# A transformer block on one core: the first batch's root on ScalarE, the second operand set copied, the weights' preparation put later

## The chip, the cores and the metric

The kernel runs on one core of one Trainium2 chip. The metric is the device time of the program in microseconds. The program is one launch that takes all inputs from DRAM and leaves the block's output there.

## What is computed

The reference, cut to what matters (B = 4 batches, T = 1024 tokens, C = 128 channels, 16 heads of 8 channels):

```python
x = x + layernorm(attn(layernorm(x), weight))
x = x + layernorm(ffn(layernorm(x), W_r, W_k, W_v, mu_r, mu_k))

def attn(x, weight):                       # b, t, c = 4, 1024, 128
    y = x.reshape(b, t, 16, 8).transpose(0, 2, 1, 3)
    scores = einsum('bhtk,bhsk->bhts', y, y) / sqrt(8)
    o = einsum('bhts,bsc->bhtc', softmax(scores), x)
    return o.transpose(0, 2, 1, 3).reshape(b, t, 16 * c) @ weight

def ffn(x, W_r, W_k, W_v, mu_r, mu_k):     # x_prev is x moved by one token
    r = sigmoid((mu_r * x + (1 - mu_r) * x_prev) @ W_r.T)
    k = square(relu((mu_k * x + (1 - mu_k) * x_prev) @ W_k.T))
    return r * (k @ W_v.T)
```

## The kernel before

The 4096 tokens are eight rows of 512. A row and a head are a step (128 steps, number j), and a step is two quads of 512 keys (256 quads, number k). All float32 products are made of float16 parts, a rounded value and what it leaves.

Every engine runs its own list, written out by hand over one loop variable k, in which the engines meet by semaphores. In iteration k the work is this:

- TensorE: `score(k)` (four 32-row matmuls into the four banks of `ps_s`), then `products(k - 4)` (twelve matmuls of 512 columns into a bank of `ps_o`), then `project(j)` (twelve matmuls of 128 columns into `ps_r`) in every second iteration. `score(k)` waits until the exponentials of quad k - 1 have left `ps_s`.
- ScalarE: `weigh(k)`, the exponentials of 128x2048 scores into `e_f`; `take_o(j)`, the rounding of a finished `ps_o` bank; `scale(j)`, four divisions of the projected step by its softmax sum.
- GpSimd: `cast(k)`, the issue of a DMA that rounds `e_f` to float16 in `e_hi`. Quad 0 is rounded by VectorE.
- VectorE: `split_quad(k - 2)`, which needs `cast` landed and gives `e_lo`; `split_o(j)`, `invert(j)`, `add(j)`.
- SyncE: all other transfers, above all the operands of the scores, which steps 4 and later read back from a scratch in DRAM. The operands of steps 0 to 3 come from TensorE transposes of `comb_s` and `comb_t`, in two sets (steps 0 and 1, steps 2 and 3).

The opening, which the change touches, does the following beside that pipeline. VectorE forms means and variances of batch 0, its inverse root (`batch_root`, L1017: an integer first guess and three rounds of three instructions, each waiting for the one before), and a negated product for ScalarE's share of the normalization (L1223, semaphore `centred`; ScalarE's `normalize_half`, L857). `first_operands(n)` on VectorE (L1075) builds set n from x: subtract, multiply, round, take the rest, square, sum, root, shift. TensorE's `first_operands(n)` (L531) transposes them, ScalarE's `take_first_s`, `take_first_t` and `take_second_t` (L861 to L876) copy them into `op_s` and `op_t`, and `score(4)` waits for the second set.

The weights of the projection are prepared in the opening as well. TensorE's `weights_less(i)` (L560, float32, 512 columns) subtracts the last row in four parts; VectorE's `weight_base(i)` (L1097) subtracts the last column; `weight_sum` on TensorE (L526), `keep_weight_sum` on ScalarE (L850) and `weight_scale` on VectorE (L1105) find a power of two; ScalarE's `weights_high` and `weights_neg` (L791, L798) and VectorE's `weights_low` (L1116) make the three float16 parts. `project(0)` (L616) waits for all of it. `step_at(k, lead)` (L247) tells in which iteration step j is projected (lead 8 on TensorE), scaled and inverted (lead 9), and added (lead 10): before, step 0 stands at lead + 1, step 1 at lead + 2, step 2 at lead + 4, and so on by two. In iteration 12 the feed-forward weights are turned by TensorE (`turn_ffn_weights`, L573) and copied by ScalarE (`turn_in_ffn_weights`, L877), on both ahead of that iteration's work for steps.

## Time and profile before

| | before |
|---|---|
| median of 3 runs | 944.18 us (943.57 to 948.45) |
| the profiled execution, its own time | 950.29 us |
| its span in the trace | 948.5 us |
| TensorE busy | 914.9 us, 96% |
| VectorE busy | 850.3 us, 90% |
| ScalarE busy | 753.4 us, 79% |
| GpSimd busy | 320.2 us, 34% |
| granted TensorE clock over the span | 0.999 |

The profile is one execution. "Busy" of an engine is the time in which it had an instruction under way. The granted clock is what the throttle let through and is not all that sets the pace: a column of one matmul form can cost twice as much in one stretch as in another, so the duration of a form is read where it stands. Views used: the page with its shares, the timeline of a stretch (start, duration, engine, line, operation, and in square brackets the idle time of the engine before it with its releaser), and the chain of work that ended last in order of time.

### The profile page before, as it was taken

The numbers are of one execution on the slowest core, as the hardware profiler recorded it, in microseconds if no ns is written. First come the engines' busy times: TensorE is split into PE (matmuls) and PEld (weight loads), VectorE is DVE, ScalarE is ACT, GpSimd is POOL, SyncE is SP. The second block draws the span as 40 slices with busy tenths as digits, with TensorE's granted clock in tenths as the row PEclk, the third lists the DMA queues.
The fourth block names the chain that finished last, engine by engine and source line by source line (L and its number), as shares of the span: only waits on it lengthen the run. The fifth ranks groups of instructions, "written<-read, shape, count | busy, mean of one in ns | idle before, by whom it ended". The sixth has DMA issues, their size and how long they took to land.

```text
span 948.5 us, 17874 instructions
## 1 busy us (share of the span) xinstructions
PE 914.9 (96%) x6065; PEld 441.9 (47%) x6065; DVE 850.3 (90%) x1117; ACT 753.4 (79%) x1048; POOL 320.2 (34%) x485
## 2 busy tenths in 40 slices
PE   3999999999999999999999999999999999999995
PEld 2444444444544444444444444544544444444453
DVE  7889898899898899989988979989889899898887
ACT  6787878788778778888778887889787978788855
POOL 2111432441143613515115282443313451153501
PEclk9999999999999999999999999999999999999999
DMA  5899999989889888999988978899988989889840
GB/s 162 195 225 188 205 197 200 226 190 204 177 173 201 163 181 174 208 193 207 185 178 179 203 157 179 176 222 202 206 173 180 188 182 188 172 179 201 174 81 24
DMA packets 98698, 173.12 MB, mean 183 GB/s; under 512 B 21040, under 2 KB 61360, under 8 KB 98608
## 3 DMA queue, kind: packets, MB, share of 16 engines
q0 software_dynamic: 36720, 133.71, 72.3%
q1 hardware_dynamic: 61888, 38.28, 14.7%
q8 instruction: 49, 0.80, 0.3%
q14 instruction: 41, 0.34, 0.1%
HBM read 27.72 MB, written 10.49 MB: 40 GB/s over the span
## 4 chain that ended last, share of the span: by engine, by line
PE 80%; issue 5%; POOL 4%; DVE 4%; DMA 4%; ACT 4%; DVEq 0%; POOLq 0%; ACTq 0%
PE ps_o L610 22%; PE ps_o L612 20%; PE ps_o L611 20%; PE ps_s L591 7%; DMA e_hi<-e_f 3%; PE ps_r L625 3%; PE ps_r L627 3%; PE ps_r L626 3%; ACT e_f L776 2%; DVE e_lo L1129 1%; POOL zT L452 1%; POOL e_hi L433 1%; PE ps_x L652 1%; PE ps_x L648 1%; POOL fnw L411 1%
## 5 line engine op out<-in xcount | busy, mean ns | idle before, releaser
L1129 DVE TENSOR_TENSOR e_lo<-e_f,e_hi 128x2048 f16<-128x2048 f32 x256 | 586.1, 2290 | 62.2 <-DMA e_hi<-e_f 62.1
L776 ACT ACTIVATE e_f<-ps_s 128x2048 f32<-128x2048 f32 x256 | 481.6, 1881 | 133.8 <-PE ps_s L591 124.4
L610 PE MATMUL ps_o<-e_hi,y_hi 128*128 128x512 f16 x1024 | 390.7, 382 | 6.3 <-DVE o_neg L1135 4.7
L612 PE MATMUL ps_o<-e_hi,y_lo 128*128 128x512 f16 x1024 | 388.1, 379 | 0.0
L611 PE MATMUL ps_o<-e_lo,y_hi 128*128 128x512 f16 x1024 | 388.1, 379 | 0.0
L433 POOL DMA_DIRECT2D e_hi<-e_f x255 | 140.9, 553 | 571.1 <-ACT e_f L776 469.8
L610 PEld LDWEIGHTS ps_o<-e_hi,y_hi 128*128 128x128 f16 x1024 | 99.7, 97 | 155.0 <-issue 56.1
L788 ACT ACTIVATE part<-ps_r,rden 128x128 f32<-128x128 f32 x508 | 144.8, 373 | 33.3 <-DVE rden L1141 32.6
L612 PEld LDWEIGHTS ps_o<-e_hi,y_lo 128*128 128x128 f16 x1024 | 100.2, 98 | 120.9
L611 PEld LDWEIGHTS ps_o<-e_lo,y_hi 128*128 128x128 f16 x1024 | 100.4, 98 | 91.5 <-issue 0.7
L591 PE MATMUL ps_s<-op_t,op_s 32*128 32x512 f16 x1024 | 102.5, 388 | 2.9 <-ACT e_f L776 2.4
L625 PE MATMUL ps_r<-w_hi,o_hi 128*128 128x128 f16 x508 | 91.6, 219 | 0.9 <-ACT part L788 0.9
L627 PE MATMUL ps_r<-w_neg,o_neg 128*128 128x128 f16 x508 | 91.6, 219 | 0.0
L626 PE MATMUL ps_r<-w_lo,o_hi 128*128 128x128 f16 x508 | 91.6, 219 | 0.0
L1151 DVE TENSOR_TENSOR acc<-acc,part 128x512 f32<-128x512 f32 x119 | 81.3, 683 | 9.4 <-ACT part L788 8.7
L1135 DVE SCALAR_TENSOR_TENSOR o_neg<-o_hi,ps_o 128x512 f16<-128x512 f16 x127 | 86.0, 677 | 2.3 <-ACT o_hi L781 2.1
L781 ACT ACTIVATE o_hi<-ps_o 128x512 f16<-128x512 f32 x127 | 76.1, 599 | 0.1
L591 PEld LDWEIGHTS ps_s<-op_t,op_s 32*128 32x128 f16 x1024 | 26.3, 91 | 66.7 <-issue 50.5
L625 PEld LDWEIGHTS ps_r<-w_hi,o_hi 128*128 128x128 f16 x508 | 49.7, 98 | 16.5 <-issue 1.9
L626 PEld LDWEIGHTS ps_r<-w_lo,o_hi 128*128 128x128 f16 x508 | 49.7, 98 | 14.6
L627 PEld LDWEIGHTS ps_r<-w_neg,o_neg 128*128 128x128 f16 x508 | 49.7, 98 | 0.0
L1141 DVE RECIPROCAL rden<-ps_r 128x4 f32<-128x4 f32 x127 | 22.4, 177 | 3.9 <-PE ps_r L627 3.9
(235 smaller groups left out, 507.4 us busy)
## 6 DMA issues: line engine op xcount, KB each, us to landing
e_hi<-e_f POOLq DMA_DIRECT2D x255, 512.0 KB, 5.1
op_t<-scr_t SPq DMA_DIRECT2D x496, 32.0 KB, 3.7
op_s<-scr_s SPq DMA_DIRECT2D x496, 16.0 KB, 3.3
scr_s<-yT SPq DMA_DIRECT2D x12, 256.0 KB, 2.9
scr_t<-yT SPq DMA_DIRECT2D x12, 256.0 KB, 5.4
out_dram<-res SPq DMA_DIRECT2D x7, 256.0 KB, 4.6
xs<-in_L_attn_x_dram SPq DMA_DIRECT2D x3, 512.0 KB, 6.2
scr_s<-eighth SPq DMA_DIRECT2D x4, 256.0 KB, 4.4
```

The source lines that it names most:

```text
L433: nc.gpsimd.dma_start(flat(e_hi[:, ring]), flat(e_f[:, k % EF_RING])).then_inc(cast_in[ring], 16)
L591: mm = nc.tensor.matmul(ps_s[:, g, :], op_s[here, slot, q * P:(q + 1) * P], op_t[here, slot, :], start=True, stop=True)
L610: nc.tensor.matmul(dst, y_hi[:, b % 2, s, :], e_hi[:, ring, g, :], start=(q == 0 and g == 0), stop=False)
L611: nc.tensor.matmul(dst, y_hi[:, b % 2, s, :], e_lo[:, ring, g, :], start=False, stop=False)
L612: mm = nc.tensor.matmul(dst, y_lo[:, b % 2, s, :], e_hi[:, ring, g, :], start=False, stop=(q == 1 and g == 3))
L625: nc.tensor.matmul(dst, o_hi[:, j % 2, here], w_hi[:, j % H, :], start=True, stop=False)
L626: nc.tensor.matmul(dst, o_hi[:, j % 2, here], w_lo[:, j % H, :], start=False, stop=False)
L627: mm = nc.tensor.matmul(dst, o_neg[:, j % 2, here], w_neg[:, j % H, :], start=False, stop=True)
L776: nc.scalar.activation(e_f[:, k % EF_RING], ps_s[:], ACT.Exp, scale=1.0 / ROOT).then_inc(weighed, 1)
L788: ins = nc.scalar.activation(part[:, j % 2, i, :], ps_r[:, i * P:(i + 1) * P], ACT.Identity, scale=rden[:, j % 2, i:i + 1])
L1129: dve.tensor_tensor(flat(e_lo[:, ring]), flat(e_f[:, k % EF_RING]), flat(e_hi[:, ring]), ALU.subtract).then_inc(split, 1)
L1135: dve.scalar_tensor_tensor(out=o_neg[:, j % 2, :], in0=o_hi[:, j % 2, :], scalar=2.0 ** O_BITS, in1=ps_o[:, j % 2, :], op0=ALU.mult, op1=A ...
```

## The change

Five things are changed.

- The inverse root of batch 0: ScalarE takes the square root from the variance, VectorE its reciprocal and one round of three instructions. Two dummy ScalarE activations are added: a Sqrt before it and an Exp behind it, ahead of `normalize_half`.
- The second operand set on VectorE is no longer computed from x but copied from batch 0's `y_hi`, `y_lo` and `shx` (six copies, `second_operands`).
- TensorE runs `products(0)` in iteration 3, ahead of the second set's transposes; `weights_less` 0 stands behind these, 1 and 2 in iteration 4, 3 in iteration 6, and `weight_sum` in iteration 7.
- The weights' further preparation is later by two iterations: VectorE's `weight_base` in iterations 3 to 6, `weight_scale` in 8, `weights_low` in 10; ScalarE's `keep_weight_sum` in 8, `weights_high` in 9, `weights_neg` in 10.
- Steps 0 and 1 are projected in iterations 10 and 11 (before 9 and 10), scaled and inverted in 11 and 12, added in 12 and 13; step 2 and all later ones stay where they were.

The diff, cut to its core:

```diff
         def weights_ps(i):
-            return (ps_o[:, 1, :], ps_o[:, 1, :], ps_r[:], ps_x[:])[i]
+            return (ps_o[:, 1, :], ps_r[:], ps_x[:], ps_r[:])[i]
         def step_at(k, lead):
-            if k == lead + 1:
-                return 0
-            return (k - lead) // 2 if k > lead and (k - lead) % 2 == 0 else None
+            if k in (lead + 2, lead + 3):
+                return k - lead - 2
+            return (k - lead) // 2 if k > lead + 3 and (k - lead) % 2 == 0 else None
...
             def weights_less(i):
                 if i == 1:
-                    pe.wait_ge(w_based, 1)
+                    pe.wait_ge(first_s_in, 2)
                 if i == 2:
-                    pe.wait_ge(first_s_in, 2)
+                    pe.wait_ge(first_t_in, 3)
                 if i == 3:
-                    pe.wait_ge(first_t_in, 3)
+                    pe.wait_ge(w_based, 2)
...
                 if k == LAG - 1:
+                    products(0)
+                    first_operands(1)
                     weights_less(0)
-                    first_operands(1)
+                if k == LAG:
                     weights_less(1)
-                if k == LAG:
                     weights_less(2)
-                    weights_less(3)
-                if 0 <= k - LAG < QUADS:
+                if 1 <= k - LAG < QUADS:
                     products(k - LAG)
                 if k == LAG + 2:
+                    weights_less(3)
+                if k == LAG + 3:
                     weight_sum()
...
+            act.wait_ge(const_ok, 1)
+            nc.scalar.activation(early[:, 0:1], consts[:, 0:1], ACT.Sqrt)
+            act.wait_ge(moment, 1)
+            nc.scalar.activation(nw[:, 3, :], mv[:, :, 1], ACT.Sqrt, bias=consts[:, 0:1]).then_inc(first_root, 1)
+            nc.scalar.activation(early[:, 1:2], consts[:, 0:1], ACT.Exp)
             normalize_half()
...
-                if k == 6:
+                if k == 8:
                     keep_weight_sum()
-                if k == 7:
+                if k == 9:
                     weights_high()
-                if k == 8:
+                if k == 10:
                     weights_neg()
...
             def batch_root():
                 step(dve.tensor_scalar(v, mv[:, :, 1], EPS, None, ALU.add))
-                step(dve.tensor_scalar(a.bitcast(I32), v.bitcast(I32), 1, None, ALU.logical_shift_right))
-                step(dve.tensor_scalar(y.bitcast(I32), a.bitcast(I32), -1.0, float(MAGIC), ALU.mult, ALU.add))
-                for _ in range(3):
-                    (three dependent instructions)
+                dve.wait_ge(first_root, 1)
+                step(dve.reciprocal(y, c))
+                (three dependent instructions, once)
...
+            def second_operands():
+                dve.tensor_copy(s[:, :, :, 0:2, :], heads(y_hi[:, 0], NB, 2))
+                dve.wait_ge(y_low, 2)
+                dve.tensor_copy(s[:, :, :, 2, :], heads(y_lo[:, 0], NB, 1)).then_inc(comb_s_ok, 1)
+                dve.tensor_copy(t[:, :, :, 0:3:2, :], heads(y_hi[:, 0], RB, 2))
+                dve.tensor_copy(t[:, :, :, 1, :], heads(y_lo[:, 0], RB, 1))
+                dve.wait_ge(shift_ok, 1)
+                dve.tensor_copy(t[:, :, :, 3, :], heads(shx, RB, 1)).then_inc(comb_t_ok, 1)
...
                 if k == 2:
-                    first_operands(1)
-                    weight_base(0)
-                    weight_base(1)
-                if k in (3, 4):
-                    weight_base(k - 1)
-                if k == 6:
+                    second_operands()
+                if 3 <= k < 7:
+                    weight_base(k - 3)
+                if k == 8:
                     weight_scale()
-                if k == 8:
+                if k == 10:
                     weights_low()
```

Further, `products` of step 1 waits for `w_based` 1 in place of 2, `weight_sum` and `keep_weight_sum` use `ps_x` in place of `ps_r`, and the tiles `yf`, `sqf` and `n2f` are kept once and not twice.

## Rows read from the trace of the kernel before

**Rows 1.** The page, busy time and share of the span by engine.

```profile
PE 914.9 (96%) x6065; PEld 441.9 (47%) x6065; DVE 850.3 (90%) x1117; ACT 753.4 (79%) x1048; POOL 320.2 (34%) x485
```

**Rows 2.** Timeline, opening: start us, duration us, engine, line, operation, idle before.

```profile
6.22 0.17 DVE L1020 TENSOR_SCALAR nw<-mv 128x8 f32<-128x8 f32 x1
...
8.64 0.17 DVE L1223 SCALAR_TENSOR_TENSOR nw<-mv,nw 128x8 f32<-128x8 f32 x1
...
8.84 1.65 ACT L857 ACTIVATE yn<-xs,nw 128x128 f32<-128x128 f32 x4 [6.84 <-DVE nw L1223]
...
12.01 0.60 ACT L870 ACTIVATE op_t<-ps_o 128x512 f16<-128x512 f16 x1 [0.64 <-PE ps_o L555]
```

**Rows 3.** Timeline, tail, ScalarE and VectorE: a table load, a root by ScalarE.

```profile
928.02 1.28 ACT L979 ACT_TABLE_LOAD   x1
...
934.04 0.30 ACT L947 ACTIVATE l_w<-l_mv,consts 128x4 f32<-128x4 f32 x1 [2.20 <-DVE l_mv L1317]
...
935.05 0.16 DVE L1334 SCALAR_TENSOR_TENSOR l_w<-l_w 128x4 f32<-128x4 f32 x1
```

**Rows 4.** Timeline, iterations 2 and 3, VectorE and TensorE.

```profile
19.19 2.28 DVE L1129 TENSOR_TENSOR e_lo<-e_f,e_hi 128x2048 f16<-128x2048 f32 x1
...
22.23 2.05 PE L570 MATMUL ps_o<-w_raw,less 128*128 128x512 f32 x2 [0.39 <-ACT shT L771]
...
23.76 0.20 DVE L1090 TENSOR_SCALAR comb_t<-n2f 128x64 f16<-128x64 f32 x1
```

**Rows 5.** Chain that ended last, 0 to 70 us: start us, us, what.

```profile
19.41 1.77 ACT e_f L776
...
24.84 0.85 PE ps_x L555 x32
...
28.14 1.06 PE ps_r L570 x2
...
30.27 0.22 PE ps_o L611
...
32.65 0.33 PE ps_s L591 x4
```

**Rows 6.** Timeline of ScalarE, 28 to 70 us.

```profile
29.97 1.90 ACT L848 ACTIVATE w_neg<-w_raw 128x2048 f16<-128x2048 f32 x1
...
44.78 1.93 ACT L801 ACTIVATE w_neg<-w_hi 128x2048 f16<-128x2048 f16 x1
...
56.09 1.14 ACT L788 ACTIVATE part<-ps_r,rden 128x128 f32<-128x128 f32 x4
...
60.34 0.38 ACT L879 ACTIVATE wT<-ps_x 128x256 f32<-128x256 f32 x1 [1.13 <-PE ps_x L577]
...
60.78 0.60 ACT L781 ACTIVATE o_hi<-ps_o 128x512 f16<-128x512 f32 x1
```

**Rows 7.** Timeline of VectorE, 28 to 70 us.

```profile
30.93 0.69 DVE L1102 TENSOR_TENSOR xs<-ps_r,w_col 128x508 f32<-128x508 f32 x1
...
39.05 0.15 DVE L1107 TENSOR_SCALAR w_bits<-w_sum 128x1 f32<-128x1 f32 x1
...
40.50 0.69 DVE L1135 SCALAR_TENSOR_TENSOR o_neg<-o_hi,ps_o 128x512 f16<-128x512 f16 x1
41.10 4.49 DVE L1129 TENSOR_TENSOR e_lo<-e_f,e_hi 128x2048 f16<-128x2048 f32 x2
45.51 2.33 DVE L1119 SCALAR_TENSOR_TENSOR w_lo<-xs,ws,w_hi 128x2032 f16<-128x2032 f32 x1
...
51.79 2.29 DVE L1129 TENSOR_TENSOR e_lo<-e_f,e_hi 128x2048 f16<-128x2048 f32 x1 [1.06 <-DMA e_hi<-e_f]
```

**Rows 8.** Tile e_hi, its DMA issues from 28 to 70 us: issue to landing.

```profile
DMA to landing us min/median/max: 4.3/5.1/6.6
```

**Rows 9.** Timeline of TensorE, 27 to 66 us, projection of step 1.

```profile
53.10 0.22 PE L625 MATMUL ps_r<-w_hi,o_hi 128*128 128x128 f16 x1 [0.89 <-ACT part L788]
...
53.86 0.39 PE L591 MATMUL ps_s<-op_t,op_s 32*128 32x512 f16 x4
```

More of the change, by code:

```diff
@@ L106, in sandwich @@
         diag = sb("diag", [P, H], F32)
-        yf = [sb(f"yf_{n}", [P, NB, SET * HS], F32) for n in range(FIRST // SET)]
-        sqf = [sb(f"sqf_{n}", [P, RB, SET * HS], F32) for n in range(FIRST // SET)]
-        n2f = [sb(f"n2f_{n}", [P, 2, RB * SET], F32) for n in range(FIRST // SET)]
+        yf = sb("yf", [P, NB, SET * HS], F32)
+        sqf = sb("sqf", [P, RB, SET * HS], F32)
+        n2f = sb("n2f", [P, 2, RB * SET], F32)
         comb_s = [sb(f"comb_s_{n}", [P, NB, SET, 4, HS], F16) for n in range(FIRST // SET)]
@@ L528, in weight_sum @@
                 pe.wait_ge(w_based, 3)
-                nc.tensor.matmul(ps_r[:, 0:1], ones[:], w_sum[:, 0:1], start=True, stop=True).then_inc(w_total, 1)
+                nc.tensor.matmul(ps_x[:, 0:1], ones[:], w_sum[:, 0:1], start=True, stop=True).then_inc(w_total, 1)
             def first_operands(n):
@@ L851, in keep_weight_sum @@
                 act.wait_ge(w_total, 1)
-                nc.scalar.activation(w_sum[:, 1:2], ps_r[:, 0:1], ACT.Copy).then_inc(w_summed, 1)
+                nc.scalar.activation(w_sum[:, 1:2], ps_x[:, 0:1], ACT.Copy).then_inc(w_summed, 1)
             def normalize_half():
@@ L1017, in batch_root @@
             def batch_root():
-                v, y, a = (nw[:, i, :] for i in range(3))
-                c = nw[:, 3, :]
+                v, y, a, c = (nw[:, i, :] for i in range(4))
                 step(dve.tensor_scalar(v, mv[:, :, 1], EPS, None, ALU.add))
-                step(dve.tensor_scalar(a.bitcast(I32), v.bitcast(I32), 1, None, ALU.logical_shift_right))
-                step(dve.tensor_scalar(y.bitcast(I32), a.bitcast(I32), -1.0, float(MAGIC), ALU.mult, ALU.add))
-                for _ in range(3):
-                    step(dve.scalar_tensor_tensor(out=a, in0=y, scalar=-0.5, in1=y, op0=ALU.mult, op1=ALU.mult))
-                    step(dve.tensor_tensor(c, a, v, ALU.mult))
-                    step(dve.scalar_tensor_tensor(out=y, in0=c, scalar=1.5, in1=y, op0=ALU.add, op1=ALU.mult))
+                dve.wait_ge(first_root, 1)
+                step(dve.reciprocal(y, c))
+                step(dve.scalar_tensor_tensor(out=a, in0=y, scalar=-0.5, in1=y, op0=ALU.mult, op1=ALU.mult))
+                step(dve.tensor_tensor(c, a, v, ALU.mult))
+                step(dve.scalar_tensor_tensor(out=y, in0=c, scalar=1.5, in1=y, op0=ALU.add, op1=ALU.mult))
             def batch_normalize(b, blocks):
@@ L1073, in batch_shift, with first_operands @@
                                   ALU.mult, ALU.add).then_inc(shift_ok, 1)
-            def first_operands(n):
+            def first_operands():
                 mean, root = mv[:, :, 0:1], nw[:, 1, :].unsqueeze(2)
-                heads = yf[n][:].rearrange("p b (h k) -> p (b h) k", k=HS)
-                near = yf[n][:, 0:RB, :].rearrange("p b (h k) -> p (b h) k", k=HS)
-                s, t = (x_[n][:].rearrange("p b h i k -> p (b h) i k") for x_ in (comb_s, comb_t))
+                heads = yf[:].rearrange("p b (h k) -> p (b h) k", k=HS)
+                near = yf[:, 0:RB, :].rearrange("p b (h k) -> p (b h) k", k=HS)
+                s, t = (x_[0][:].rearrange("p b h i k -> p (b h) i k") for x_ in (comb_s, comb_t))
@@ L1080, in first_operands @@
                 n_s, n_t = NB * SET, RB * SET
-                step(dve.tensor_tensor(yf[n][:], xs[:, 0:NB, n * SET * HS:(n + 1) * SET * HS], mean.to_broadcast([P, NB, SET * HS]), ALU.subtract))
-                step(dve.tensor_tensor(yf[n][:], yf[n][:], root.to_broadcast([P, NB, SET * HS]), ALU.mult))
+                step(dve.tensor_tensor(yf[:], xs[:, 0:NB, 0:SET * HS], mean.to_broadcast([P, NB, SET * HS]), ALU.subtract))
+                step(dve.tensor_tensor(yf[:], yf[:], root.to_broadcast([P, NB, SET * HS]), ALU.mult))
@@ L1087, in first_operands @@
                 dve.tensor_tensor(t[:, :, 1, :], near, t[:, :, 0, :], ALU.subtract)
-                step(dve.tensor_reduce(n2f[n][:, 0, :], sqf[n][:].rearrange("p b (h k) -> p (b h) k", k=HS), AX.X, ALU.add))
-                near_root(n2f[n][:, 1, :], n2f[n][:, 0, :])
-                dve.tensor_scalar(t[:, :, 3, :], n2f[n][:, 1, :].unsqueeze(2).to_broadcast([P, n_t, HS]), -SLACK * LONGEST,
+                step(dve.tensor_reduce(n2f[:, 0, :], sqf[:].rearrange("p b (h k) -> p (b h) k", k=HS), AX.X, ALU.add))
@@ L1091, in first_operands, with heads @@
+                near_root(n2f[:, 1, :], n2f[:, 0, :])
+                dve.tensor_scalar(t[:, :, 3, :], n2f[:, 1, :].unsqueeze(2).to_broadcast([P, n_t, HS]), -SLACK * LONGEST,
                                   TOP * ROOT, ALU.mult, ALU.add).then_inc(comb_t_ok, 1)
+            def second_operands():
+                here = slice(SET * HS, FIRST * HS)
+                s, t = comb_s[1], comb_t[1]
+                def heads(x_, blocks, n):
+                    x_ = x_[:, 0:blocks, here].rearrange("p b (h k) -> p b h k", k=HS)
+                    return x_.unsqueeze(3).to_broadcast([P, blocks, SET, n, HS]) if n > 1 else x_
+                dve.tensor_copy(s[:, :, :, 0:2, :], heads(y_hi[:, 0], NB, 2))
[5 more added lines that the diff above has]
+                dve.tensor_copy(t[:, :, :, 3, :], heads(shx, RB, 1)).then_inc(comb_t_ok, 1)
```

10 lines of the change are left out of this document (5 added, 5 removed).

## The prediction, made before the changed kernel ran

> **What bounds the kernel now.** I read the page's shares first: TensorE is busy for 96% of the span, VectorE for 90%, ScalarE for 79% [rows 1]. TensorE sets the pace of the loop and has the same work after the change as before it. So a microsecond counts only where TensorE stands idle or runs its columns slowly, and both happen mostly in the first 60 us, which is where all edits lie. Next I read the timeline of the opening to see what releases what, then the chain of work for the ends of matmul groups, then the lists of ScalarE and VectorE from 28 to 70 us, because there the weights are prepared. What the reader is to see in them: up to 22 us a chain through all engines, in which each exponential (1.77) is followed by another ScalarE copy before the next score [rows 5]; from 22.2 us TensorE without gaps; and at 53.10 one wait of 0.89 us for ScalarE's `scale(0)` [rows 9].
>
> **The root (gain 1.2 us).** VectorE's root and the step behind it run from 6.22 to a last start at 8.64, twelve intervals of 0.2 [rows 2]. The tail has the new form: ScalarE's root starts at 934.04, the last of VectorE's four steps at 935.05 [rows 3], so one more step, `centred`, would start 1.2 us after the root. ScalarE can begin at 6.24; `centred` starts at 7.45, against 8.64: 1.19 us earlier. Behind the root ScalarE must load the Exp table, 1.28 us [rows 3], and run a small Exp (some 0.2): root 6.24 to 6.54, load to 7.83, free at 8.0, against a start of `normalize_half` at 8.84 [rows 2]. Its four instructions (1.65) end at 9.65, just when the first transposed operands, also 1.2 earlier, are there. The first Sqrt table load falls in the idle time before 6 us. So `op_t` of step 0, at 12.01 before [rows 2], comes at 10.8, and everything up to iteration 3 is 1.2 us earlier. The load is hidden as long as it ends before 8.84, 0.8 us later than I expect; beyond that it delays `normalize_half` and, with it, ScalarE's first copy. VectorE's new wait for the root holds up its whole opening list, and is in the 1.2 us.
>
> The Trainium skill, "ScalarE: Activation LUTs", section "What ACT_TABLE_LOAD costs", counts a drain of about 1.38 us on top of the 1.28 us load. In the tail the next activation follows the load at once. By the page ScalarE would be free at 9.4 and the opening would gain some 0.4 us in place of 1.2, the total being 0.8 us worse; I go by the row.
>
> **The second operand set (nothing).** The old one filled VectorE from 21.4, the end of its first split, to 23.96 [rows 4]. Six copies without waits between them cost at most half of that, 1.3 us; at 0.2 each, 1.2. But `products(0)` now stands ahead of the transposes on TensorE and covers either. The gain on VectorE is idle time: its next split waits for the DMA of quad 1. What the copies wait for (the low parts, the shift) is done before 20 us.
>
> **Products(0) first (iterations 3 to 8: gain 0.8 us in all, the 1.2 included).** Score(3) moves from 21.23 to 20.0, the first split ends at 20.2, and products(0) starts at 20.6, so TensorE is continuously busy 1.6 us earlier than at 22.23 [rows 4]. At which speed? The float32 pass of `weights_less` took 2.05 at 22.23 [rows 4] and 1.06 at 28.14 [rows 5]: columns cost double until about 27.9 though the granted clock reads full, that is 1.2 and then 2.4 GHz. Continuous work from 22.2 brought the fast pace some 5.6 us later. Products cost 0.22 a matmul at the fast pace [rows 5], twelve are 2.6; at the slow one 5.2. I let them all run slowly, 20.6 to 25.8, and the fast pace begin there. Bounds: 23.7 (gain 1 us) and 28.0 (loss 0.9).
>
> From there, at the fast pace (transposes 0.3 and 0.43, half of 0.85 [rows 5]; `weights_less` 1.0; score 0.33 [rows 5]):
> - Transposes to 26.5, `weights_less(0)` to 27.5. ScalarE copies the set (0.6 and 0.95) to 27.7. Score(4) at 27.75, against 27.63 before. `weights_less` 1 and 2 to 30.1, score(5) at 30.1, products(1) to 33.0.
> - ScalarE: exponentials of quad 4 from 28.1 to 29.9, the squares of the weights (1.90 and the read of the sum [rows 6]) to 31.9, quad 5 to 33.7. So score(6) waits 0.8 us, to 33.8: before, products(0) lay in iteration 4 and covered the squares.
> - Products(2) to 36.7, `weights_less(3)` to 37.7, score(7), products(3), the sum, score(8) at 40.9. Before it was at 41.77. The lead is 0.8 to 0.9 us. The new waits of `weights_less` 1 to 3 (copies in, two bases done at 31.4) are over when their turn comes.
>
> **The weights come late for project(0) (loss 3.2 us net).** I walk VectorE's list back from `weights_low`, now behind split(8) in iteration 10, while project(0) stands behind products(6) of the same iteration. Quad 8's exponentials end 1.85 + 0.33 behind the start of score(8), at 43.0. Its DMA needs 0.3 to issue and 4.3 to 6.6 to land [rows 8]; with 5.7 it is there at 49.1. VectorE alone comes to the same: split(6) from 42.5 (its own DMA), 2.2 each [rows 7]; `weight_scale` 1.4, from 39.05 to 40.50 [rows 7]; split_o 0.6; split(7): free at 48.9. Split(8) runs to 51.3, `weights_low` (2.25 [rows 7]) to 53.57. ScalarE: `weights_high` from 46.1 to 48.1, quad 10 to 49.9, `weights_neg` (1.83 [rows 6]) to 51.7, so VectorE is last. TensorE: score(8), products 4 to 6 and two scores end at 49.65. **Project(0) starts at 53.63 after 4.0 us of idle time.** Before, `weights_low` stood behind split(6) and project(0) behind products(5), one quad more between them: idle 0.4 us for score(9) and 0.4 for project(0). With landings of 4.3 the new idle time is 3.3, with 6.6 it is 4.2.
>
> **Project(1) (no change).** Before it waited 0.89 for `scale(0)` [rows 9]; now score(11) to the end of `scale(0)` is 0.4 + 1.8 + 1.13 [rows 6] and products(7) ends 0.7 us sooner. I take 0.7.
>
> **Project(2) (loss 2.2 us).** This wait is new. In iteration 12 project(2) needs step 1 scaled; before, that was done in iteration 11. Now `scale(1)` is in ScalarE's list of iteration 12 behind `turn_in_ffn_weights`, which itself waits for TensorE's `turn_ffn_weights`, the last thing ahead of project(2). So from the end of these transposes TensorE waits for 0.44 of copies, 0.55 of `take_o` (60.34 to 60.78 and 0.60 [rows 6]), 1.13 of `scale` and two hand-overs: 2.25 us, whatever the times before it. Behind ScalarE's `scale(1)` nothing else is queued that TensorE lacks, and from step 3 on the two orders are the same.
>
> **The sum.** Score(8) is 0.8 earlier. Idle time from there to project(2) is 4.0 + 0.7 + 2.2 = 6.9, before 0.4 + 0.4 + 0.9 = 1.7. The end moves by -0.8 + 5.2 - 0.2 (roundings) = +4.2 us; I take +4.0, since two of the terms (fast pace, landing) have more room below than above. TensorE has no slack later to win it back, SyncE's loads for steps 4 and 5 are 1.2 us earlier and land before scores 8 and 10 need them. The profiled span 948.5 would become 952.5 and its execution 950.29 some 954.3; this execution lay 6.1 above the median of the runs shown, and I put the 4.0 on the median: **948.2 us**, 0.42% slower.
>
> **The rivals.**
> - **Low clock in the stall, slower (0.14).** TensorE stands idle for 4 us before project(0). If its clock falls back to 1.2 GHz, the work behind runs at double cost for about as long as in the opening: 5.6 us of it hold 2.8 us of loss, 951.0. For it: before 22 us, with idle times under 1 us, the pace was slow all the time. Against it: no idle time as long stands in the trace of before in a fast stretch. The Trainium skill, "TensorE: Matmul & The Clock Gate", section "HAM oscillation — how this bites in real kernels", says that a wait in the middle of a kernel can make the gate close again; by it this rival would come true and the sum be +6.8. No row here can show it.
> - **The slow pace lasts to 28 us (0.12).** Then products(0) and what follows run slowly till 28.0: +0.9, 949.1.
> - **The weights are in time, not slower than before (0.14).** The place is VectorE's list of iterations 6 to 10. If the landings are all at the short end and VectorE has no gap from 23 us on, `weights_low` ends 26 us later (eight splits of 2.2, four bases of 0.8, 1.4, 1.2, 2.25), at 49 us, before TensorE ends products(6). Then project(1)'s 0.7 and project(2)'s 2.2 are left against the lead of 0.8 and the 1.7 of idle time that before had: +0.4, less the 0.2 of roundings, 944.4, which is before's time. It decides from the point where the DMAs of quads 4 to 8 land within 4 us of their exponentials' end. Against it: none did from 28 to 70 us [rows 8], and split(8) waited for its own even at the slower pace [rows 7].
> - **Root or copies do nothing (0.06).** If ScalarE's table load delays `normalize_half`, the 1.2 goes and the time is 949.2.
>
> **How the numbers follow.** The forecast, both stalls at about these sizes, has 0.54; with its bounds (pace from 23.7 or 28.0, landing 4.3 to 6.6) it reaches from +2.3 to +5.1, 946.5 to 949.3. The range 944.5 to 951.5 takes in the other cases but for the tails of the first and third rival, and a microsecond of difference between medians. A measurement of this kernel can tell about 0.5%, 4.7 us, from no change. Slower by over that: the first rival whole, half of the two at 949.1 and 949.2, and a quarter of the forecast: 0.38. Faster by over 4.7 needs more than the whole gain of the opening: 0.04. Within: 0.58.
>
> **What would show it.** The root: `centred` at 7.45, `normalize_half` at about 8.0. The pace: the first products at 20.6 with 0.43 between matmuls. Iteration 6: a 0.8 us wait of ScalarE's squares for score(6). Project(0): the first L625 row with some 4 us of idle time and VectorE's w_lo or its releaser before it. Project(2): the third with 2.2 us released by `part`. The forecast is wrong if project(0) finds its weights ready, or if TensorE is found idle again later by less than before.

## The result, and the profile after

| | before | changed |
|---|---|---|
| first set of runs: median, number | 946.11 us, 7 runs (943.57 to 948.52) | 955.5 us, 7 runs (952.4 to 957.48) |
| ratio, 95% interval | | 1.009 (1.0066 to 1.0113) |
| the same kernels in two later sets | 948.02 (35 runs); 946.94 (23 runs) | 952.91 (12 runs); 954.71 (6 runs) |
| ratios, 95% intervals | | 1.0043 (1.0026 to 1.0061); 1.0075 (1.0054 to 1.0095) |
| span of the first profile | 948.5 us | 953.7 us |
| granted clock over the span | 0.999 | 0.992 |

The changed kernel is slower, by 0.4 to 0.9% in three sets, 0.7% in their mean: some 6.5 us. The intervals of the first two don't overlap, so the interval of one set does not hold all the scatter. I had forecast 4.0 us more, 948.2 us, with a range to 951.5. All three medians lie above that range.

The page of the changed kernel, its share row, beside [rows 1]:

```profile
PE 917.7 (96%) x6065; PEld 443.7 (47%) x6065; DVE 849.3 (89%) x1104; ACT 754.9 (79%) x1052; POOL 310.1 (33%) x485
```

TensorE is busy for as much of the span as before, and VectorE for less. In the line of the granted clock by slices (40 of 23.8 us) the third slice, from 47.7 to 71.5 us, stands at 8, and so does the last:

```profile
PEclk9989999999999999999999999999999999999998
```

Finer, the busy time of each engine in stretches of 2 us of the changed kernel, from 48 to 60 us (columns: stretch, its length, busy time and count of PE, PEld, DVE, ACT, POOL, then the granted clock, the DMA share and GB/s):

```profile
48.00:50.00 2.00, 1.57 (x8) 0.49 (x5) 1.58 (x2) 2.00 (x2) 0.28 (x1) 1.00 1.18 311
50.00:52.00 2.00, 0.00 (x0) 0.00 (x0) 2.00 (x2) 1.22 (x1) 0.24 (x1) 0.96 1.08 221
52.00:54.00 2.00, 0.74 (x8) 0.77 (x9) 1.01 (x1) 0.00 (x0) 0.00 (x0) 0.50 1.11 234
54.00:56.00 2.00, 2.00 (x13) 0.82 (x12) 0.57 (x1) 1.20 (x2) 0.00 (x0) 0.50 0.81 230
56.00:58.00 2.00, 2.00 (x6) 0.76 (x5) 2.00 (x3) 2.00 (x5) 0.53 (x1) 0.50 0.31 80
58.00:60.00 2.00, 2.00 (x16) 1.10 (x15) 0.39 (x1) 0.21 (x1) 0.00 (x0) 0.83 1.00 247
```

TensorE stands idle from 49.4 to 53.3 us, and from 51.9 to 58.7 us its clock is at 1.2 GHz (0.50) and not at 2.4. So the fall comes during the wait, and 5.4 us of work behind the wait run slowly. The timeline of TensorE shows what stands around it (start us, duration us, engine, line, operation, idle before it with its releaser):

```profile
48.76 0.38 PE L610 MATMUL ps_o<-e_hi,y_hi 128*128 128x512 f16 x1
...
53.26 0.26 PE L625 MATMUL ps_r<-w_hi,o_hi 128*128 128x128 f16 x1 [3.69 <-DVE w_lo L1140]
...
55.18 0.61 PE L610 MATMUL ps_o<-e_hi,y_hi 128*128 128x512 f16 x1
...
56.43 0.63 PE L610 MATMUL ps_o<-e_hi,y_hi 128*128 128x512 f16 x1
...
58.84 0.38 PE L610 MATMUL ps_o<-e_hi,y_hi 128*128 128x512 f16 x1
...
65.93 0.22 PE L625 MATMUL ps_r<-w_hi,o_hi 128*128 128x128 f16 x1 [2.25 <-ACT part L790]
```

Project(0) waits 3.7 us from the modelled end of the last product (3.9 us from the point where one more product could have started) for the low part of the weights. The products behind it come 0.43 us apart and not 0.22. Project(2) waits 2.25 us for `scale(1)`. In the kernel before project(2) waited for nothing there, and project(1) waited 0.89 us for `scale(0)` [rows 9]. VectorE's rows for the low part and its list around it, beside [rows 7]:

```profile
43.23 0.15 DVE L1128 TENSOR_SCALAR w_bits<-w_sum 128x1 f32<-128x1 f32 x1
...
48.47 2.29 DVE L1150 TENSOR_TENSOR e_lo<-e_f,e_hi 128x2048 f16<-128x2048 f32 x1 [0.42 <-DMA e_hi<-e_f]
50.67 2.33 DVE L1140 SCALAR_TENSOR_TENSOR w_lo<-xs,ws,w_hi 128x2032 f16<-128x2032 f32 x1
```

The opening, beside [rows 2] first ScalarE's timeline (root, its table load, the normalization), then VectorE's (`centred`, the first and the last of the copies):

```profile
6.16 0.30 ACT L887 ACTIVATE nw<-mv,consts 128x8 f32<-128x8 f32 x1 [2.52 <-DVE mv L1021]
6.48 1.28 ACT L888 ACT_TABLE_LOAD   x1
7.77 0.20 ACT L888 ACTIVATE early<-consts 128x1 f32<-128x1 f32 x1
7.88 1.63 ACT L859 ACTIVATE yn<-xs,nw 128x128 f32<-128x128 f32 x4
```

VectorE's timeline of the same stretch:

```profile
7.40 0.17 DVE L1244 SCALAR_TENSOR_TENSOR nw<-mv,nw 128x8 f32<-128x8 f32 x1
...
20.14 0.22 DVE L1106 COPY comb_s<-y_hi 128x256 f16<-128x256 f16 x1
...
20.57 0.18 DVE L1112 COPY comb_t<-shx 128x64 f16<-128x64 f16 x1
```

**A ruler for the opening.** Each kernel's trace has one activation per quad, `e_f<-ps_s`. Its start for quad 16, less that of before (71.09 us), tells what the opening gained or lost, free of what happens later. For the changed kernel it is +5.78 us in the first profile, +6.18 and +5.58 in the two others. The zero is a single profile of before, in which the fast pace came late: e6 has the same work on TensorE up to 25.6 us and was 0.95 us ahead from there (see below). So a reading is good to about 1 us. From quad 16 to the last quad single executions scatter by some us either way, as the paragraph on the loop shows, and the medians of before itself in five sets (946.11 to 948.02) lie 1.9 us apart.

### The profile page after: what moved, and what is told of

Its sections match the earlier page's. It is cut to its first block, busy times and chain, and to the rows that moved or that the text cites. A ratio compares the mean times of both kernels' runs of the same rounds, so it can differ in the third digit from the quotient of the medians.

```text
span 953.7 us, 17866 instructions
## 1 busy us (share of the span) xinstructions
PE 917.7 (96%) x6065; PEld 443.7 (47%) x6065; DVE 849.3 (89%) x1104; ACT 754.9 (79%) x1052; POOL 310.1 (33%) x485
## 4 chain that ended last, share of the span: by engine, by line
PE 75%; issue 6%; DVE 6%; DMA 6%; POOL 3%; ACT 3%; DVEq 0%; POOLq 0%; ACTq 0%
PE ps_o L610 21%; PE ps_o L611 19%; PE ps_o L612 18%; PE ps_s L591 7%; DMA e_hi<-e_f 5%; PE ps_r L625 3%; PE ps_r L627 2%; PE ps_r L626 2%; ACT e_f L778 2%; DVE e_lo L1150 2%; POOL zT L452 1%; PE ps_x L642 1%; PE ps_x L648 1%; POOL e_hi L433 1%; PE ps_x L652 1%
## 5 line engine op out<-in xcount | busy, mean ns | idle before, releaser
L790 ACT ACTIVATE part<-ps_r,rden 128x128 f32<-128x128 f32 x508 | 144.7, 373 | 28.3 <-DVE rden L1162 27.9
L1172 DVE TENSOR_TENSOR acc<-acc,part 128x512 f32<-128x512 f32 x119 | 83.9, 705 | 10.4 <-ACT part L790 9.4
```

The lines of the kernel that those rows point to most:

```text
L790: ins = nc.scalar.activation(part[:, j % 2, i, :], ps_r[:, i * P:(i + 1) * P], ACT.Identity, scale=rden[:, j % 2, i:i + 1])
```

## The experiments

Each set of kernels ran on one chip together with the kernel before. The table gathers them; the ratio is to before in the same set, with its 95% interval, and the last column is the ruler, in us, from one profile each.

| run | median us | ratio | quad 16 against before |
|---|---|---|---|
| changed, first | 955.5 | 1.0090 (1.0066 to 1.0113) | +5.78 |
| e13, changed again | 952.91 | 1.0043 (1.0026 to 1.0061) | +6.18 |
| e15, changed, third | 954.71 | 1.0075 (1.0054 to 1.0095) | +5.58 |
| e1, wait filled | 950.2 | 1.0032 (1.0019 to 1.0045) | +4.96 |
| e2, weights sooner | 950.15 | 1.0039 (1.0022 to 1.0056) | +2.55 |
| e3, turn later | 952.56 | 1.0052 (1.0035 to 1.0069) | +4.75 |
| e4, order alone | 955.31 | 1.0088 (1.0064 to 1.0112) | +8.37 |
| e5, root alone | 945.71 | 0.9983 (0.9969 to 0.9997) | -1.22 |
| e8, e2 and e3 | 946.34 | 0.9999 (0.9984 to 1.0014) | -0.39 |
| e9, e8 and scale first | 946.94 | 1.0003 (0.9986 to 1.0021) | -0.64 |
| e10, old times | 946.81 | 0.9997 (0.9982 to 1.0012) | -0.81 |
| e12, both waits filled | 947.08 | 0.9993 (0.9979 to 1.0008) | +4.32 |
| e16, the same again | 948.67 | 1.0020 (1.0005 to 1.0036) | +3.86 |
| e6, copies alone | 947.64 | 0.9994 (0.9976 to 1.0012) | -0.95 |
| e11, root, scale first | 945.81 | 0.9982 (0.9965 to 0.9999) | -2.52 |
| e14, e11, clock early | 944.03 | 0.9969 (0.9956 to 0.9981) | -3.78 |

### e1: the wait of project(0) filled with idle matmuls

```diff
+                if k == LAG + 6:
+                    pe.wait_ge(w_summed, 1)
+                    for _ in range(16):
+                        nc.tensor.matmul(ps_x[:], ident16[:], y_hi[:, 0, 0:RB, :]..., start=True, stop=True)
```

> The changed kernel with sixteen idle matmuls of 512 columns put on TensorE ahead of project(0), where it waits 3.9 us for the weights; they write a bank that nobody reads then. If the clock fell because of that wait, it stays high (granted clock 1.0 from 50 to 60 us in place of 0.66), the work behind runs at 0.22 a matmul, and the time is 2.8 us under the changed kernel's, some 952.5 where that one has 955.3. If the clock has nothing to do with the wait, or the weights alone matter, the time stays or rises, since the idle matmuls could only delay project(0).

Measured: 950.2 us, ratio 1.0032. Stretches of 2 us from 62 us on (columns as above):

```profile
62.00:64.00 2.00, 0.57 (x11) 0.60 (x12) 0.69 (x1) 1.29 (x5) 0.00 (x0) 1.00 1.06 208
64.00:66.00 2.00, 2.00 (x13) 0.77 (x11) 1.70 (x3) 1.36 (x1) 0.00 (x0) 0.63 0.70 220
66.00:68.00 2.00, 2.00 (x6) 0.70 (x5) 2.00 (x4) 1.55 (x5) 0.53 (x1) 0.52 0.24 32
```

TensorE's timeline there:

```profile
63.43 0.22 PE L625 MATMUL ps_r<-w_hi,o_hi 128*128 128x128 f16 x1 [2.25 <-ACT part L795]
...
65.77 0.63 PE L610 MATMUL ps_o<-e_hi,y_hi 128*128 128x512 f16 x1
```

The work behind project(0) ran at the fast pace, as expected; but the clock fell all the same, 1.1 us after the end of project(2)'s wait. So the first fall follows from the first wait, and behind a wait of 2.25 us there was another. The opening is only 0.8 us better than the changed kernel's. The first low stretch had cost 2.5 us; the new one costs 1.7, and project(1) now waits, which makes 0.8 more, since ScalarE no longer has the slow products to finish behind. The other 0.7 us are an earlier fast pace in the opening and a slightly shorter wait. The time fell by more than the opening tells; this comes up again under what is open.

### e2: the weights' preparation sooner

```diff
-                if k == 8:
+                if k == 7:
                     keep_weight_sum()
-                if k == 9:
+                if k == 8:
                     weights_high()
-                if k == 10:
+                if k == 9:
                     weights_neg()
...
-                if k == 8:
+                if k == 7:
                     weight_scale()
-                if k == 10:
+                if k == 8:
                     weights_low()
```

> The changed kernel with the weights' preparation drawn forward in the lists of ScalarE and VectorE: sum kept and scale in iteration 7, high part in 8, negated part in 9, low part in 8 (changed kernel: 8, 9, 10, 10). If the wait for the low part is the main loss, both the 3.9 us of waiting and the 2.8 us of slow clock go, less some 0.6 us for a later exponential: 6 us under the changed kernel, at 949 or a little less. If the loss lies in the reordered products and transposes, less than 2 us is won.

Measured: 950.15 us, ratio 1.0039. Project(0) waits for nothing any more; project(2) does, and the clock falls behind it. TensorE's rows:

```profile
50.21 0.22 PE L625 MATMUL ps_r<-w_hi,o_hi 128*128 128x128 f16 x1
...
61.11 0.22 PE L625 MATMUL ps_r<-w_hi,o_hi 128*128 128x128 f16 x1 [2.25 <-ACT part L790]
...
62.46 0.61 PE L610 MATMUL ps_o<-e_hi,y_hi 128*128 128x512 f16 x1
```

The opening gained 3.2 us and not 6. The wait (3.9) and the slow work behind it (2.5) went. Against this stand 0.9 for a later exponential and a later split (waits of 0.48 and 0.32), 0.8 for project(1), which now waits as in e1, and 1.6 for a low stretch that now comes behind project(2)'s wait.

### e3: the feed-forward weights turned one iteration later

```diff
-                if k == 12:
+                if k == 13:
                     turn_ffn_weights()
...
-                if k == 12:
+                if k == 13:
                     turn_in_ffn_weights()
```

> The changed kernel with the feed-forward weights' transposes and copies moved from iteration 12 to 13 on TensorE and ScalarE. If project(2) waits because scale(1) stands behind them, its wait falls from 2.25 to 0.9 us: 1.3 us under the changed kernel. If project(2) waits for scale(1) whatever stands before it, no change.

Measured: 952.56 us, ratio 1.0052; quad 16 is 1.03 us sooner than in the changed kernel. TensorE's row of project(2):

```profile
64.57 0.22 PE L625 MATMUL ps_r<-w_hi,o_hi 128*128 128x128 f16 x1 [0.89 <-ACT part L790]
```

The wait is 0.89 us in place of 2.25, as expected. So 1.36 of the 2.25 us are the turned weights that stood ahead of `scale(1)`; the rest is `take_o` and `scale` themselves. The ruler shows 1.03 and not 1.3, since in this profile quad 4 was already 0.2 us later.

### e4: the order alone

The root and the second operand set as in the kernel before, all else as changed.

> The changed kernel with the root and the second operand set as before, that is the reordering alone. If the reordering makes the whole loss and the root gains 1.2 us, this is 1.2 us over the changed kernel: some 10 us over the kernel before if that has 946. The copies are hidden and give nothing. If the root or the copies cost something, it is under the changed kernel.

Measured: 955.31 us, ratio 1.0088, quad 16 at +8.37: 2.6 us more than the changed kernel. Score(8) starts 1.6 us later: the root's 1.2, as expected, and 0.4 since the fast pace came that much later in the opening. The wait for the weights is 1.55 us longer, since the DMA of quad 8 took 6.9 us to land and 5.4 in the changed kernel; VectorE's row shows the wait for it:

```profile
51.62 2.29 DVE L1132 TENSOR_TENSOR e_lo<-e_f,e_hi 128x2048 f16<-128x2048 f32 x1 [1.93 <-DMA e_hi<-e_f]
```

Since more of the low stretch fell into this longer wait, it cost 2.0 and not 2.5 us. The time is that of the changed kernel's first set and 0.6 to 2.4 us over its two others. Together with e5 and e6, in which root and copies alone lose nothing, this puts the whole loss on the order.

### e5: the root alone

Only `batch_root`, ScalarE's root and the two dummy activations, on the kernel before.

> The kernel before with the root of the first batch on ScalarE and nothing else of the change. If the root's 1.2 us are carried to the end, 1.2 us under the kernel before. If they are swallowed by the wait for the slow columns or for VectorE, no change; if the clock's rise comes at a fixed time, less than 1.2.

Measured: 945.71 us against 946.98, ratio 0.9983; the exponentials of every quad from 0 to 30 start 1.21 to 1.23 us sooner. The root's gain is kept whole through the opening, and the time agrees with it.

### e6: the copies alone

`second_operands` in place of `first_operands(1)`, on the kernel before.

> The kernel before with the second operand set copied and nothing else. If TensorE's weights_less(0) covers VectorE's operand work in both forms, no change: the exponentials of quad 4 start at 28.2 as before. If the copies free VectorE in time for the splits, a gain of up to 1.4 us.

Measured: 947.64 us, ratio 0.9994. The exponentials of quad 4 start 0.95 us sooner, which I had not expected, yet not for the copies' sake: in this execution the clock rose sooner. TensorE's second pass of the weights took 1.30 us, where it took 2.08 in the profile of before; both began at 25.6, and the first pass and the transposes ahead of it are the same in both ([rows 4] has the first). The same shows between e5 and e11, which have the same work up to here: the pass took 2.08 in e5 and 1.13 us in e11.

```profile
22.18 2.05 PE L570 MATMUL ps_o<-w_raw,less 128*128 128x512 f32 x2 [0.39 <-ACT shT L771]
...
25.57 1.30 PE L570 MATMUL ps_o<-w_raw,less 128*128 128x512 f32 x2
```

### e8 and e9: both waits shortened; scale(1) ahead of take_o(3)

e8 has the edits of e2 and e3. e9 adds:

```diff
+                if k == 12:
+                    scale(1)
                 j = (k - LAG - 2) // 2
                 if (k - LAG - 2) % 2 == 0 and 0 <= j < LAST_STEP:
                     take_o(j)
                 j = step_at(k, LAG + 5)
-                if j is not None and j < LAST_STEP - 1:
+                if j is not None and j < LAST_STEP - 1 and k != 12:
                     scale(j)
```

> The changed kernel with the weights' preparation drawn forward (as in the run of that name) and the feed-forward weights' turn in iteration 13. If the two waits, and the clock that falls after each, are the whole loss, the low clock from 60 to 66 us is gone, project(2) waits 0.9 us, and the exponentials of quad 14 start 1.1 us earlier than before: 945 to 946. If the clock falls without a wait, or the wait only moves on, it stays at 949 to 950.

Measured: 946.34 us, ratio 0.9999. The granted clock is 1.00 from 20 to 70 us and project(2) waits 0.90 us:

```profile
60.00:70.00 10.00, 10.00 (x68) 4.80 (x65) 8.11 (x10) 8.03 (x13) 1.20 (x3) 1.00 0.85 184
```

TensorE's timeline, the row of project(2):

```profile
59.43 0.22 PE L625 MATMUL ps_r<-w_hi,o_hi 128*128 128x128 f16 x1 [0.90 <-ACT part L790]
```

With both waits short, the whole loss is gone. Quad 16 is 6.2 us sooner than in the changed kernel, and 0.4 us sooner than in before, where I had expected 1.1: the waits of 0.48, 0.32 and 0.6 us that e2 has are still there.

> As the last, and scale(1) ahead of take_o(3) in ScalarE's list of iteration 12. Project(2)'s wait falls from 0.9 to 0.4 us; take_o(3) and VectorE's split of it come 1.1 us later and project(3) does not need them yet. 0.5 us under the last; if the later take_o holds up TensorE, the same or more.

Measured: 946.94 us, ratio 1.0003; quad 16 0.25 us sooner than e8's and not 0.5. Project(2) waits 0.4 us, which is the expected 0.5 less, but in this profile quad 4 was 0.2 us later than in e8. The difference can't be told in the times.

### e10: nothing put later

The changed kernel with the weights' preparation and steps 0 and 1 at the iterations of before: root, copies, and products(0) first.

> The changed kernel with the weights' preparation and steps 0 and 1 at the old iterations: root, copies and products(0) first, and nothing put later. If products(0) first is worth something in itself, it is more than the root's 1.2 us under the kernel before; by the lead of 1.3 us that the changed kernel has at score(8), and project(0) waiting little, some 1.5 to 2 us. If only the root counts, 1.2. If the squares' 0.7 us wait and a late VectorE take the lead back, nothing or worse than before.

Measured: 946.81 us, ratio 0.9997; quad 16 at -0.81. Waits of TensorE from 26 to 75 us (waiting for whom: us in total, times, longest):

```profile
PE ps_r L625 <- ACT part L789: 0.9, 1, 0.9
PE ps_s L591 <- ACT e_f L777: 0.6, 1, 0.6
PE ps_r L625 <- DVE w_lo L1139: 0.5, 1, 0.5
```

Less than the root's 1.22, by no more than the ruler can tell. So products(0) first gains nothing that can be seen: score(6) waits 0.6 us behind the squares of the weights, and project(0) 0.5 us for the low part. The expectation of 1.5 to 2 us was wrong.

### e12 and e16: both waits filled

Sixteen idle matmuls ahead of project(0) and nine ahead of project(2), the latter behind a wait that score(13) has anyway, in a bank of `ps_s`.

> The changed kernel with idle matmuls in both waits: sixteen ahead of project(0), nine ahead of project(2). In the run with the first alone the clock fell after the second wait instead. If each fall follows from a wait, the clock is at full from 24 us to the tail and the exponentials of quad 14 start 2.8 us sooner than in the changed kernel, 3.0 us after the kernel before; the time is 3 us over that one. If the clock falls by something else, a low stretch remains between 50 and 70 us.

Measured: 947.08 us, ratio 0.9993. The granted clock, stretches of 4 us:

```profile
48.00:52.00 4.00, 4.00 (x21) 1.80 (x19) 3.48 (x3) 3.16 (x2) 0.53 (x1) 1.00 1.13 266
52.00:56.00 4.00, 3.40 (x28) 1.66 (x27) 2.19 (x4) 1.51 (x2) 0.00 (x0) 1.00 1.00 241
...
64.00:68.00 4.00, 3.69 (x29) 1.88 (x28) 2.68 (x4) 2.65 (x6) 0.16 (x1) 1.00 0.57 146
```

No low stretch is left before the tail, so each fall follows from a wait. Quad 16 is 1.5 us sooner than in the changed kernel's first profile and not 2.8: the slow work cost 2.5, project(0) waited 0.4 us longer in this execution, and with a fast clock project(1) loses 0.8 us which the slow products had hidden. But the ratio is that of a kernel 0.7 us faster than before, 5 us better than this opening accounts for, so I ran it again.

> The changed kernel with both waits filled, again. By its first profile (quad 14 late by 4.3 us) 1.004; by its first times 0.999. If its usual opening is 3 us late, as I expected of it, 1.003. If it repeats 0.999, the opening alone does not tell a kernel's time to better than 3 us.

Measured: 948.67 us, ratio 1.0020, quad 16 at +3.86. The two ratios have a mean of 1.0007. The opening of +3.9 to +4.3 us would give 1.004. This stays open: the kernel with both waits filled is some 3.5 us better than its opening tells (5 and 2 in the two sets), and two profiles of it don't show where.

### e13 and e15: the changed kernel again

> The changed kernel once more, beside the others on one chip. If its 9 us over the kernel before are its own, 955 to 956 again. The trace accounts for 5.8 us at quad 14 and 1.4 us in the tail; if the rest is scatter of its seven runs, 953 to 954. The waits of 3.9 and 2.25 us and the low clock from 52 to 59 us stand in the second profile as in the first.

> The changed kernel a third time. If the loss is its opening (5.8 to 6.2 us at quad 14 in the two profiles) and the rest is scatter, the ratio lies at 1.006, between the first two results (1.009 and 1.004). If it has a loss in the loop of its own, 1.009 again.

Measured: 952.91 and 954.71 us, 1.0043 and 1.0075. The mean of the three ratios is 1.0069, 6.5 us, where the openings have 5.8 on average. The second profile, in stretches of 2 us, shows that the falls are not the same in every execution:

```profile
54.00:56.00 2.00, 2.00 (x10) 0.74 (x7) 1.41 (x3) 2.00 (x2) 0.00 (x0) 0.62 0.73 218
56.00:58.00 2.00, 2.00 (x7) 0.67 (x6) 1.54 (x1) 1.35 (x5) 0.53 (x1) 0.53 0.37 96
64.00:66.00 2.00, 1.16 (x12) 1.19 (x12) 0.39 (x1) 0.69 (x3) 0.00 (x0) 0.68 1.00 228
66.00:68.00 2.00, 2.00 (x10) 0.55 (x9) 1.69 (x3) 1.13 (x1) 0.00 (x0) 0.50 0.27 93
```

TensorE's timeline, project(0) and project(2):

```profile
53.03 0.22 PE L625 MATMUL ps_r<-w_hi,o_hi 128*128 128x128 f16 x1 [3.81 <-DVE w_lo L1140]
...
64.84 0.26 PE L625 MATMUL ps_r<-w_hi,o_hi 128*128 128x128 f16 x1 [2.25 <-ACT part L790]
```

Here the wait of project(0) is 3.8 us, project(0) itself still runs fast (0.22), the clock falls only 1.5 us later, and it falls once more at the end of the 2.25 us wait, where it did not in the first and third profile. Both low stretches last 3.4 us, where that of the first and third profile lasts 6.8; the slow work costs 3.2 us in all here and 2.5 and 2.4 there.

### e11 and e14: a faster kernel than either

e11 is e5 with `scale(0)` ahead of `take_o(2)` in ScalarE's iteration 10 (as in e9, with k == 10). e14 adds idle matmuls in TensorE's idle times of the opening:

```diff
+            def keep_busy(bank, n):
+                for _ in range(n):
+                    nc.tensor.matmul(bank[:], ident16[:], eighth[:, 0:BANK], start=True, stop=True)
...
                 if k == 0:
                     turn_y(0, 0)
+                    keep_busy(ps_x, 2)
                     turn_top(0)
                 if k == 1:
                     turn_y(0, 1)
                     spread_top(0)
+                    pe.wait_ge(first_t_in, 2)
+                    keep_busy(ps_r, 2)
                 if k == 2:
                     turn_shift(0)
+                    keep_busy(ps_r, 2)
                 if k == LAG - 1:
+                    keep_busy(ps_r, 1)
                     weights_less(0)
```

> The kernel before with the root on ScalarE, and scale(0) ahead of take_o(2) in ScalarE's list of iteration 10. The root gives 1.2 us, the shorter wait of project(1) (0.9 to 0.4) another 0.5: quad 14 starts 1.7 us sooner than before, some 945.2. If the wait is taken up by the later take_o(2), it is 1.2.

Measured: 945.81 us against 948.02, ratio 0.9982. Project(1) waits 0.4 us in place of 0.89; quad 16 is at -2.52, of which 1.2 are the root, 0.5 the shorter wait, and 0.8 an earlier rise of the clock in this execution, as in e6.

> The run with the root on ScalarE and scale(0) first, with seven idle matmuls of 512 columns put into TensorE's idle times between 13 and 22 us. If the slow columns before 26 to 28 us are the cost of a clock that rises only with TensorE's activity, the clock rises earlier, weights_less(0) takes 1.0 in place of 2.05 us and the transposes half, and quad 4's exponentials start up to 2 us sooner; the time is 2 us under that run's, 4 under the kernel before. If the idle matmuls only get in the way of the scores, it is slower than that run by a few tenths.

Measured: 944.03 us against 946.94, ratio 0.9969 (0.9956 to 0.9981). TensorE's passes of the weights:

```profile
14.29 0.39 PE L596 MATMUL ps_s<-op_t,op_s 32*128 32x512 f16 x4
...
21.04 1.10 PE L575 MATMUL ps_o<-w_raw,less 128*128 128x512 f32 x2 [0.29 <-ACT shT L781]
...
23.39 1.13 PE L575 MATMUL ps_o<-w_raw,less 128*128 128x512 f32 x2 [0.16 <-DVE xs L1117]
```

The scores and passes are fast from 14 us on, when two of the seven idle matmuls had begun; 2.05 us of [rows 4] are 1.10. The scores up to quad 3 are not late. Quad 16 is at -3.78, 1.3 us better than e11 and 2.6 us better than the root alone. This is the fastest of all the kernels, 2.9 us under the one before and 11 us under the changed one's 954.7 in the same set. Against e11 alone, which ran in another set, the two intervals overlap. It has neither the new order nor the copies.

## Why the prediction was wrong

**The root: right.** Forecast: 1.19 us, `centred` at 7.45, ScalarE free at 8.0. Measured: `centred` at 7.40, `normalize_half` at 7.88, first exponential 1.24 us sooner; in e5 the gain is there at quad 16 and in the time. The drain behind a table load that the Trainium skill counts ("ScalarE: Activation LUTs", "What ACT_TABLE_LOAD costs") does not show here either: the load ends at 7.76 and the next activation starts at 7.77.

**The copies: right.** They take 0.6 us where the set took 2.6, from 20.14 to 20.75, and nobody waits for them.

**Products(0) first: right in kind, better than forecast.** They began at 20.54 with 0.43 between them (forecast 20.6). The fast pace came at 24.6 and not at 25.8, inside the bounds; score(8) stood at 40.43 (forecast 40.9), a lead of 1.3 and not 0.8 us. The wait of score(6) behind the squares was 0.65 us (0.8). In e10 a part of this lead was lost again by project(0), and nothing was left of it beyond the root's gain.

```profile
20.54 0.61 PE L610 MATMUL ps_o<-e_hi,y_hi 128*128 128x512 f16 x1
...
24.35 0.48 PE L610 MATMUL ps_o<-e_hi,y_hi 128*128 128x512 f16 x1
...
33.41 0.40 PE L591 MATMUL ps_s<-op_t,op_s 32*128 32x512 f16 x4 [0.65 <-ACT e_f L778]
```

**Project(0)'s wait: right.** Forecast 4.0 us, from 49.65 to 53.63. Measured 3.9, from 49.4 to 53.3, released by the low part. Forecast of VectorE's list: split(8) from 49.1, `weights_low` to 53.57; measured 48.47 and 53.0. The bound was wrong, though: by the same walk a landing of 6.6 us puts everything 0.9 later and makes a wait of 4.9 us, not 4.2. In e4 the landing took 6.9 and the wait 5.2 us.

**Project(1)'s wait: wrong by 0.7, hidden.** It waited for nothing, since the slow products gave ScalarE the time. Where the products ahead of it ran fast (e1, e2, e8, e12) it is 0.6 us.

**Project(2)'s wait: right.** Forecast 2.25, measured 2.25, and e3 shows that what is new in it comes from the turned weights ahead of `scale(1)`.

**The clock: this is the step that failed.** The sum took the work behind the new wait of project(0) at the fast pace, so it had nothing for the clock. I had the fall as a rival with 0.14, at a price of 2.8 us for 5.6 us of slow work. It came true in all three profiles of the changed kernel: in the first the work from 53.3 to 58.7 us ran slowly and took 2.5 us more, in the others 3.2 and 2.4. The price was about right and the chance was not. I had set the idle time of the new wait against a trace that had no such wait in a fast stretch, and took this absence as evidence that the clock would stay. The Trainium skill, "TensorE: Matmul & The Clock Gate", section "HAM oscillation — how this bites in real kernels", speaks of a wait in a running kernel after which the gate has closed again; the traces here agree with it, by 3.7 us of waiting and a clock of 0.50 behind it. That the low clock comes from the waits is shown by e1, e8 and e12.

From score(8) to score(13) TensorE now takes 26.3 us, from 40.43 to 66.69, and took 19.1 (41.77 to 60.91): 7.1 more. Taken from start to start, less what the same work takes where nothing waits, the waits make 3.9 + 2.4 against 1.7 in before (four waits, the longest 1.1): 4.6. The slow clock makes 2.5. Less the lead of 1.3 that is the 5.8 us of quad 16. The terms that I did forecast come to 3.3 in this way (forecast 4.2), so without the clock the opening would have lost less than I said.

**The range.** Two more errors lie in it. The median of three runs on which I put the loss, 944.18, was low: with 23 to 35 runs before has 946.6 to 948.0. That is 2.8 us or so. And the rival would have given 951.0 on that base, near the end of my range; on 947 it is 953.8, between the later sets (952.9, 954.7). The first set's 955.5 has some 2 us more, and its cause is not shown. In the tail the clock was low in some executions, which made it 1.4 us longer in the first profile than in that of before. The chain, the feed-forward network of the last row:

```profile
941.80 0.70 PE ps_r L727 x2
...
943.02 1.20 PE ps_s L727 x2
```

In one and the same step the half that began at 941.80 took 0.70 and the one at 943.02 took 1.20. The tail from the last quad on is 40.2 or 40.3 us in the profile of before and in e2, e3, e4 and e13, 41.3 to 42.1 in the others, e5 and e14 among them, so it is no property of the change.

**The loop.** From quad 14 to the last the profiles have between 836.5 (e1) and 844.0 us (e9), and before has 843.9. The differences arise between quads 80 and 120 and between 140 and 160. In e9, 290 to 365 us, ScalarE waited for VectorE's `rden` for 5.7 us in total, in e1 for 1.9. What sets this off in one execution and not in the next was not tried. It is why single profiles can't be compared by their spans.

**What is open.** Why the kernel with both waits filled is better than its opening, by some 3.5 us in the mean of two sets. Ratio and ruler agree within 1.1 us for every other run except two kernels: the changed one itself (its ratios are 2.7 us above, 2.1 below and 1.5 above what its openings tell) and e1, which also has idle matmuls in a wait and is 1.9 us better than its opening. Also open is whether the first set's 1.009 had a cause beyond scatter.

## What to carry to other kernels

A step that is put later in one engine's list must be walked through all the lists it needs: here the weights' low part had one quad less between it and its user, and `scale(1)` came to stand behind a copy that waits for the very engine that waits for it. When a change opens an idle time of nearly 4 us on TensorE, as here, put slow work behind it (3.4 to 5.4 us here) into the sum as the likely case, not as a rival; for an idle time of about 2 us give it an even chance (four of the eight of 1.9 to 2.25 us here). Where TensorE must wait anyway, idle matmuls on a free bank can keep or raise the clock; here they held up nothing that could be seen. Put a forecast on a median of many runs: three runs were 3 us off here, as much as the effect's main terms.

## What the hardware showed

- A wait of 3.7 to 5.2 us on TensorE was followed by a low clock in all five profiles that have one (three of the changed kernel, e3, e4). A wait of 2.25 us was followed by one in e1, e2 and e13, but not in e4 and not in the first and third profile of the changed kernel. Waits of 0.9 us were not followed by one anywhere.
- The loop has one such fall too, in one profile. In e4 a wait of 1.86 us for VectorE was followed by one, 0.1 us after its end, while a wait of 2.12 us in e13, at 432.6, was not:

```profile
565.80 0.57 PE L611 MATMUL ps_o<-e_hi,y_hi 128*128 128x512 f16 x1 [1.86 <-DVE o_neg L1138]
```

The clock of e4 behind it:

```profile
566.00:570.00 4.00, 4.00 (x12) 1.51 (x11) 4.00 (x3) 3.66 (x7) 2.49 (x3) 0.59 0.83 171
```

- The fall came during the wait in the first and third profile of the changed kernel, and 1.5 us after its end in the second. The clock stayed low for 3.4 or 6.8 us. What counts is the work that falls into this time: 1.5 to 1.7 us were lost by each stretch of 3.4 us, 2.0 to 2.5 by each of 6.8 us, whose first part fell into the wait.
- Filling the waits kept the clock high (e12, e16), and with seven idle matmuls between 13 and 21 us the columns were fast from 14 us on (e14, one profile), where in all other profiles that came between 23.6 and 27.9 us. The rise varies from execution to execution of the same work: passes that began at 25.6 took 2.08 in one and 1.30 us in the other.
- The granted clock in the profile reads 1.00 in the opening although the columns cost double there, while it reads 0.50 in the later falls. The traces have no record of the clock before its first rise, at 27.9 us in before, 24.6 in the changed kernel and 13.7 in e14, which is where the columns become fast; the views print 1.00 for the time without a record. So the durations of one form tell the pace in the opening.
